# A two-layer feed-forward and scan kernel: GpSimd's blocks spread one to a step, a sum and the transposes issued earlier

## The reference

```python
x = x + 0.5 * ffn(_layernorm(x))     # first feed-forward phase
x = x + mixer(_layernorm(x))         # gated scan over the 1024 positions
x = x + 0.5 * ffn(_layernorm(x))     # second feed-forward phase

def ffn(x):                          # H = 256, F = 1024
    h = (x - mu) * rsqrt(var + EPS) * ln_gamma + ln_beta
    y = silu(h @ w1 + fc1_bias)      # w1 = (q - 128) * scale, a scale for each 128 rows
    z = y @ w2 + fc2_bias            # w2 likewise
    return x + 0.5 * z
```

## Time and profile before

| | us |
|---|---|
| median of 3 runs (lowest, highest) | 741.46 (740.76, 741.74) |
| the profiled execution | 739.66 |
| its span in the profile | 737.8 |
| first feed-forward phase, mixer, second feed-forward phase (rough) | 20 to 306, to 446, to 738 |

### The profile page before, as it was taken

One profiled execution on the slowest core, in us unless ns is written; L12 is line 12 of the kernel. 1 busy time (PEld: TensorE's weight loads), 2 busy tenths in 40 slices (PEclk: granted clock), 3 DMA queues, 4 the chain that ended last, 5 costly groups with the idle time before them and its releaser, 6 DMA issues. The chain is left out here.

```text
span 737.8 us, 13716 instructions
## 1 busy us (share of the span) xinstructions
PE 698.3 (95%) x3250; PEld 539.9 (73%) x3250; DVE 627.5 (85%) x1216; ACT 637.0 (86%) x1052; POOL 623.6 (85%) x800
## 2 busy tenths in 40 slices
PE   4899999999999999989999997999999999999996
PEld 3577777777777777767788874777777777777774
DVE  6599998999999988688777785999999998999886
ACT  4889899998998999688888878889999899998984
POOL 5899999999999988767666658999999999999963
PEclk9999999999999999999999999999999999999999
DMA  8640000000000000000000000001110000000001
GB/s 259 205 140 1 1 0 0 0 0 0 0 0 0 1 1 0 1 1 1 0 0 0 1 0 1 2 28 35 44 37 28 28 29 28 28 30 28 30 30 59
DMA packets 19674, 19.96 MB, mean 27 GB/s; under 512 B 1532, under 2 KB 19378, under 8 KB 19634
## 3 DMA queue, kind: packets, MB, share of 16 engines
q1 hardware_dynamic: 19536, 19.48, 8.3%
q10 hardware_dynamic: 98, 0.02, 0.0%
HBM read 11.11 MB, written 8.39 MB: 26 GB/s over the span
## 5 line engine op out<-in xcount | busy, mean ns | idle before, releaser
L690 DVE SCALAR_TENSOR_TENSOR z_acc<-ps_z,cols,z_acc 128x512 f32<-128x512 f32 x448 | 322.5, 747 | 55.2 <-PE ps_z L902 24.5
L393 POOL TENSOR_TENSOR g_lo<-g_full,g_hi 128x512 fp32r<-128x512 f32 x256 | 329.5, 1293 | 36.2 <-ACT g_hi L562 35.4
L902 PE MATMUL ps_z<-g_hi,q_sb 128*128 128x512 f32 x512 | 210.8, 412 | 16.1 <-ACT z_acc L552 8.4
L560 ACT ACTIVATE g_full<-ps_fc,safe_scale 128x512 f32<-128x512 f32 x256 | 178.6, 698 | 51.9 <-PE ps_fc L902 38.6
L902 PE MATMUL ps_fc<-h_hi,q_sb 128*128 128x512 f32 x512 | 215.1, 420 | 4.8 <-ACT ps_fc L545 4.1
L902 PE MATMUL ps_fc<-h_lo,q_sb 128*128 128x512 f32 x512 | 203.6, 398 | 0.0
L902 PE MATMUL ps_z<-g_lo,q_sb 128*128 128x512 f32 x512 | 202.1, 395 | 0.0
L562 ACT ACTIVATE g_hi<-ps_fc,safe_scale 128x512 fp32r<-128x512 f32 x256 | 178.5, 697 | 0.0
L902 PEld LDWEIGHTS ps_z<-g_hi,q_sb 128*128 128x128 f32 x512 | 96.0, 187 | 69.5 <-ACT z_acc L552 22.4
L545 ACT ACTIVATE ps_fc<-ps_fc,bias,ratio 128x512 f32<-128x512 f32 x160 | 122.2, 764 | 1.4 <-DVE bias L785 1.4
L902 PEld LDWEIGHTS ps_fc<-h_hi,q_sb 128*128 128x128 f32 x512 | 97.2, 190 | 25.8 <-ACT ps_fc L545 4.1
(11 more groups left out here) (105 smaller groups left out, 813.8 us busy)
## 6 DMA issues: line engine op xcount, KB each, us to landing
resid<-in_L_attn_x SPq DMA_DIRECT2D x15, 512.0 KB, 4.2
out_x<-resid SPq DMA_DIRECT2D x15, 512.0 KB, 2.9
q_int<-in_L_ffn_fc_q SPq DMA_DIRECT2D x4, 512.0 KB, 7.0
resid<-in_L_attn_x SPq DMA_DIRECT2D x2, 256.0 KB, 3.0
out_x<-resid SPq DMA_DIRECT2D x2, 256.0 KB, 2.8
wd_sb<-in_L_attn_Wd SPq DMA_DIRECT2D x1, 256.0 KB
wy_raw<-in_L_attn_Wy SPq DMA_DIRECT2D x2, 64.0 KB
wab_sb<-in_L_attn_Wa SPq DMA_DIRECT2D x1, 64.0 KB
```

Source lines behind the costliest of these rows:

```text
L393: nc.gpsimd.tensor_tensor(g_lo[:, g % 4, :], g_full[:, g % 2, :], g_hi[:, g % 4, :].bitcast(F32), ALU.subtract).then_inc(g_ready, 1)
L560: nc.scalar.activation(g_full[:, g % 2, :], bank, ACT.Silu, scale=scale)
L690: nc.vector.scalar_tensor_tensor(out=z, in0=bank_of(g, n, par), scalar=col(R_S2 + KC * g + n), in1=z, op0=ALU.mult, op1=ALU.add).then_inc( ...
L902: last = nc.tensor.matmul(out, w, v, start=start and i == 0, stop=stop and i == len(pairs) - 1, skip_group_check=not start)
```

## The change

Nothing is computed otherwise, and no instruction is added or taken away on GpSimd, PE or DMA; the scaling of one group goes to other engines group by group, but five groups of a tile stay on ACT and three on DVE.

- GpSimd: `residual` is no longer four blocks in one step (step 1), but one block in each of the steps 0 to 3. `rsqrt` goes from step 2 to step 4. The three blocks of `normalise` go from steps 5, 5, 6 to steps 5, 6, 7, and `xhat_ready` is given in step 7.
- PE: the two halves of `turn` go from steps 1 and 3 to steps 0 and 2, `turn_back` from steps 5 and 6 to steps 4 and 5. DVE's `lower_h` and `add_ffn`, which follow them, go a step forward too, and `variance` goes to step 7.
- ACT: `first_sum` for n = 0 is issued before `silu(3)` and not behind it, for n = 1 right behind it. ACT scales groups 1, 3, 5, 6, 7 and DVE 0, 2, 4; before it was 0, 2, 4, 5, 6 and 1, 3, 7.
- `g_full` has four slots, and `silu` waits for `g_low` of four groups back instead of two.
- Tile 0 has entries of its own: `residual` in steps 2 and 3, `normalise` in steps 6 and 7.

```diff
     BANKS = tuple(tuple((FC * KC * par + KC * g + n) % 3 for g in range(FC)) for par in range(2) for n in range(KC))
 
 
-    SCALED_ON_ACT = (0, 2, 4, 5, 6)
-    SCALED_ON_DVE = (1, 3, 7)
+    SCALED_ON_ACT = (1, 3, 5, 6, 7)
+    SCALED_ON_DVE = (0, 2, 4)
     TINY = 2.0 ** -60
 
 
     STATISTICS_AT = 4
-    VARIANCE_AT = 5
-    RESIDUAL_AT = (4, 1, 1)
-    RSQRT_AT = (5, 2, 2)
-    NORMALISE_AT = ((6, 7), (5, 6), (5, 6))
-    TURN_AT = ((3, 5), (1, 3), (1, 3))
-    TURN_OUT_AT = ((3, 5), (1, 3), (1, 3))
-    H_LOWER_AT = ((4, 6), (2, 4), (2, 4))
-    XN_LOWER_AT = (4, 6)
-    FIRST_SUM_AT = (4, 5)
-    TURN_BACK_AT = ((), (5, 6), (5, 6))
-    ADD_AT = ((), (6, 7), (6, 7))
+    VARIANCE_AT = 7
+    RESIDUAL_AT = ({2: (0, 1), 3: (2, 3)},) + ({0: (0,), 1: (1,), 2: (2,), 3: (3,)},) * 2
+    RSQRT_AT = (5, 4, 4)
+    NORMALISE_AT = ({6: (0, 1), 7: (2,)},) + ({5: (0,), 6: (1,), 7: (2,)},) * 2
+    TURN_AT = ((3, 5), (1, 3), (0, 2))
+    TURN_OUT_AT = ((3, 5), (1, 3), (0, 2))
+    H_LOWER_AT = ((4, 6), (2, 4), (1, 3))
+    XN_LOWER_AT = (3, 5)
+    TURN_BACK_AT = ((), (5, 6), (4, 5))
+    ADD_AT = ((), (6, 7), (5, 6))
     assert KC == 2 and 2 * N == P and S == 2 * TILE and FC == 8 and NT % 2 == 0
...
-            def normalise(ln, t, blocks, last_part=True):
+            def normalise(ln, t, blocks, complete):
...
-                if last_part:
+                if complete:
                     last.then_inc(xhat_ready, 1)
...
-            def residual(ln, t, shares):
-
-                pool.wait_ge(xhat_ready, ln + 1)
-                wait(pool, xhat_half_ready, shares)
-                for a in range(SUB):
+            def residual(ln, t, shares, blocks=range(SUB)):
+
+                if blocks[0] == 0:
+                    pool.wait_ge(xhat_ready, ln + 1)
+                    wait(pool, xhat_half_ready, shares)
+                for a in blocks:
                     last = nc.gpsimd.tensor_scalar(resid[:, t, a, :], resid[:, t, a, :], res_scale[:, a:a + 1],
                                                    shift[:, 1, a:a + 1], ALU.mult, ALU.add)
-                last.then_inc(resid_scaled, 1)
+                if blocks[-1] == SUB - 1:
+                    last.then_inc(resid_scaled, 1)
...
-                nc.gpsimd.tensor_tensor(g_lo[:, g % 4, :], g_full[:, g % 2, :], g_hi[:, g % 4, :].bitcast(F32),
+                nc.gpsimd.tensor_tensor(g_lo[:, g % 4, :], g_full[:, g % 4, :], g_hi[:, g % 4, :].bitcast(F32),
...
-                        if behind >= 1 and f == RESIDUAL_AT[before]:
-                            residual(ln + 1, t + 1, share(ln + 1, ff0))
+                        if behind >= 1 and f in residual_at:
+                            residual(ln + 1, t + 1, share(ln + 1, ff0), residual_at[f])
...
-                                normalise(ln + 2, t2, MOST[normalise_at.index(f)], f == normalise_at[1])
+                                normalise(ln + 2, t2, normalise_at[f], f == FC - 1)
...
-                wait(act, g_ready, FC * ff + (g - 1))
-                nc.scalar.activation(g_full[:, g % 2, :], bank, ACT.Silu, scale=scale)
+                wait(act, g_ready, FC * ff + (g - 3))
+                nc.scalar.activation(g_full[:, g % 4, :], bank, ACT.Silu, scale=scale)
...
-                        if f == FIRST_SUM_AT[1]:
-                            first_sum(ff, par, 1)
                         if f in SCALED_ON_ACT:
                             scale_half(ff, f)
+                        if f == LAG:
+                            first_sum(ff, par, 0)
                         if f >= 1:
                             silu(ff, f - 1, par)
...
-                        if f == FIRST_SUM_AT[0]:
-                            first_sum(ff, par, 0)
+                        if f == LAG:
+                            first_sum(ff, par, 1)
```

More of the change, by code:

```diff
@@ L57, in macaron_kernel @@
     out_view = out.rearrange("b s d -> (b s) d").rearrange("(t a p) d -> p t a d", p=P, a=SUB)
-    MOST, REST = (range(0, 2), range(2, 3)), range(3, 4)
+    REST = (3,)
     R_S1, R_B1 = 0, KC * FC
@@ L124, in macaron_kernel @@
         drive = sb("drive", [N, 2, TILE])
-        g_full = sb("g_full", [P, 2, TILE])
+        g_full = sb("g_full", [P, 4, TILE])
         g_hi = sb("g_hi", [P, 4, TILE], F32R)
@@ L133, in macaron_kernel @@
         xn_hi, xn_lo = h_hi, h_lo
-        c_sb, state = g_full[0:N, :, :], z_acc[0:N, 0, :, :]
+        c_sb, state = g_full[0:N, 0:2, :], z_acc[0:N, 0, :, :]
         scratch = q1_int[:, :, :].bitcast(F32).rearrange("p k f -> p (k f)").rearrange("p (b n) -> p b n", n=TILE)
@@ L442, in tile @@
                     ff, ln = t + ff0, t + ln0
-                    normalise_at = NORMALISE_AT[before]
+                    residual_at, normalise_at = RESIDUAL_AT[before], NORMALISE_AT[before]
                     for f in range(FC):
@@ L451, in tile @@
                         if not before and f == 1:
-                            normalise(ln0 + 1, 1, halves[0])
+                            normalise(ln0 + 1, 1, halves[0], True)
                         if ff0 == 0 and not behind and f in XN_LOWER_AT:
                             xn_low(0, 0, XN_LOWER_AT.index(f))
-                        if behind >= 1 and f == RESIDUAL_AT[before]:
-                            residual(ln + 1, t + 1, share(ln + 1, ff0))
+                        if behind >= 1 and f in residual_at:
+                            residual(ln + 1, t + 1, share(ln + 1, ff0), residual_at[f])
                         if behind >= 2 or ff0 == 0:
@@ L466, in feed_forward @@
                     rsqrt(ln0, True)
-                    normalise(ln0, 0, halves[0])
+                    normalise(ln0, 0, halves[0], True)
                     prepare_columns()
@@ L541, in scale_half @@
                 act.wait_ge(half_done, FC * ff + (f + 1))
-                if type(ff) is int and ff == 0 and f == 0:
+                if type(ff) is int and ff == 0 and f == SCALED_ON_ACT[0]:
                     act.wait_ge(bias_ready, 1)
```

## The result

The changed kernel takes **814.82 us** (median of 4 runs, 814.47 to 815.71), the kernel before 741.6 (740.76 to 742.08): a ratio of 1.099, 95% interval 1.0971 to 1.101. It is slower by 73 us. 781 was forecast, with 761 to 791 as the range, so the direction was right, and the size fell outside.

The account below looks back on a forecast made before the run. The prediction took a loop through GpSimd, PE and ACT, 17.65 us a tile, to bound the kernel. Profiled 739.66 + 41.0 for 24 tiles - 1.2 for the ends = 779.5; with 1.8 for the median, 781 us, range 761 to 791.

Parts of the forecast that it names:

- rival D: At PE's stops of 2.9 us a tile, TensorE's clock falls: up to +6 us a tile, 925 us; chance 0.05.
- The loop: From GpSimd's third `xhat` block through PE's transposes, ACT and GpSimd to the next: 19.36 us a tile, +1.71.
- The ends: Tile 14 of each phase +5.8 us, tiles 0 and 1 -7.0: together -1.2 us, trusted to 4.
- The side paths priced at nothing: ACT's silus and scalings, DVE's additions with `lower_h`, the turn-back's wait for `add_ffn`: no cost, covered by wait or backlog.
- Rival A: The shorter loop, through GpSimd's `g_lo`(0) alone, binds: 18.65 us a tile, 764 us; chance 0.13.
- Rival B: Third `xhat` block ready before PE's transposes, GpSimd simply full: 16.9 us a tile, 716 us; chance 0.06.

Follow-up runs that it names:

- the two moves: Changed kernel with the transposes back in steps 1 and 3 and GpSimd's `rsqrt` and `xhat` blocks one step earlier: 714.66 us, ratio 0.965 to the kernel before.

## Why the prediction was wrong

**The step that failed** is rival D, "TensorE's clock falls", and with it the sum, which takes PE's matmuls 0.233 us apart in all 24 periods. I gave D 0.05 because no wait with a row in the trace before was as long as the expected one, 2.9 us against 2.15; about 2.9 that trace could say nothing, and I took its silence for a reason against. Measured: idle waits of 2.3 to 2.6 us, shorter than expected, and yet slow matmuls behind fifteen of 24, each of these periods 1.5 us longer. The filled wait shows that with the clock kept up 26 us go. The price I put on D, up to 6 us a tile and 925 us in all, was too high, since the slow stretch lasts 3 to 4 us and not 7.5, and since nine tiles were spared; D had the right mechanism and the wrong size and chance. The Trainium skill, TensorE: Matmul & The Clock Gate, section Why this matters for your kernels, warned against such gaps; the runs agree with it, in fifteen of 24 tiles.

**The loop was right.** At full clock its period is 19.54 measured for 19.36 predicted, and each piece is there: the wait of PE at the transposes, GpSimd idle before `g_lo`(0) and again before `g_lo`(2), never behind `rsqrt`. Putting the transposes back takes all of the loss away. Neither half of the meeting does it alone: the transposes early cost 10 us, GpSimd late 2, both together, in the changed kernel, 48.7 at full clock. The period is off by 0.18 us, in 24 tiles 4 us: 0.10 us more than summed up to `g_lo`(0), and another 0.10 up to `g_lo`(3).

**The ends** were put at -1.2 us, to be trusted to 4. At full clock the kernel is 48.7 us above the kernel before, and 24 periods that are 1.8 to 1.9 longer make 44 to 45 of it, so the ends are about +4, some 5 us off; no run tells which of their terms failed. Period and ends together make 789 for 781, inside the range; the clock put it outside.

**The side paths priced at nothing** stayed there: the period at full clock leaves 0.18 us for all of them, and PE's long waits end with the block.

**Rival A**, 18.65, is out: GpSimd does wait again behind `g_lo`(1). **Rival B**, GpSimd full, did not come about here, but gave the time of another kernel, in which its condition holds: 716 for 714.7 measured, once the block comes ahead of the transposes. The gap closing that the Trainium skill asks for (Perfetto Trace Analysis, section Optimization Strategy) gives 26 us there, but it took the two moves to get it; the parts of this change that close gaps, taken alone, gave 0.

What stays open: why GpSimd's new order alone alternates between two periods and loses 2 us; what decides in which tiles the clock falls, since the length of the wait alone doesn't; and what the new scaling groups and the later `variance` do, which no run has alone.

## What to carry to other kernels

When work is moved earlier on one engine and its input later on another, add up the loop that the two now make, through every engine, before counting the waits that go. Here 1.95 us of slack met a move of 1.86 on one side and of 1.81 and more on the other, and what the other edits are worth could not show. Count the slack to the point at which the loop closes, not to the first consumer: by the transposes alone the block was still almost in time, but `g_lo`(0) behind them came 0.54 us later, and that cost 10 us. And where a new wait of PE is longer than any that the trace has at full clock, price the fall of the clock as a likely case, by what one fall costs and in how many tiles; a shorter wait is no proof that it stays up.

## What the runs showed of the hardware

In the changed kernel the granted clock fell to its lower level (0.53 and 0.51 in the two stretches read) behind fifteen of 24 PE waits of 2.3 to 2.6 us and cost 1.5 us each time: matmuls started 0.43 us apart for 0.23, for 3 to 4 us. Waits of the same length left it full in the other nine, and at the start of the second phase one wait of 1.77 us had a fall behind it and another of 1.77 us had none. So how long a wait is does not by itself say whether the clock falls. Filling the wait with matmuls that compute nothing kept the clock at 1.00 and made the kernel 26 us faster.
